# A macaron layer on one core: the opening stages of the kernel laid out anew

## Chip, cores and metric

One core of a Trainium2 chip runs the whole kernel in one launch. The metric is the device time in microseconds (us) of that core; the time of a kernel is the median of its runs. Lower is better.

## What is computed

The input x has 8 batches of 512 rows with 512 columns, all in float32. Each batch goes through three residual steps:

```
x = x + 0.5 * ffn(layernorm(x), W1, W2, W3)
x = x + attention(layernorm(x), qkv_w, proj_w, norm weights, s)
x = x + 0.5 * ffn(layernorm(x), W1, W2, W3)

ffn(x):  hidden = silu(x @ W1.T) * (x @ W3.T)      # 512 x 2048
         hidden = fwht(hidden)                     # Walsh-Hadamard transform over 2048
         return hidden @ W2.T
```

The attention is a chunked one with a decay per head (16 heads of 32, chunks of 128 rows), and its two weight matrices are rounded to -1, 0 and 1 by their mean absolute value.

## The kernel before

**Numbers.** A float32 operand is held as two float16 tiles, a high part and a low part; a product takes three matmuls (high by high, high by low, low by high), or two where the other side is exact. A group of the gate or the linear product is 12 matmuls of 128x128 by 128x512 (four tiles of the contraction by three). ScalarE makes the high part and VectorE the low part, nearly everywhere.

**The transform is moved into W2.** Since the Walsh-Hadamard transform is linear, the kernel transforms W2 once, in the opening: three butterfly stages on GpSimd (step `fly`, lines 696 to 718), then a high and a low part (`w2split`), a turn by DMA transposes into w2t, and on TensorE the last stages, as products with +1/-1 matrices over pairs of tiles (`w2pair`, lines 1342 to 1361). Pair i fills two PSUM banks with eight matmuls; ScalarE and VectorE copy them back to w2t as high and low parts (lines 791 to 795 and 1022 to 1027). Before, the pairs alternate between two bank pairs: a_bank, and g_bank with l_bank.

**One list of steps.** All engines walk the same list STEPS, written out by the Python functions first_steps and feed_forward; each engine issues its own instructions for the steps that concern it, in order, and waits on semaphores. A dictionary of slots says which steps stand at which place: slot 2j comes between gate and lin of hidden tile j, slot 2j+1 after lin j. The 16 feed-forward passes have the numbers n = 0 to 15. The opening is first_steps (lines 334 to 393):

1. W1 and W3 are loaded in 16 chunks of 128 rows (both matrices) through a stage of four. Per chunk, `wsum` takes squares on ScalarE (line 751), `wscale` makes power-of-two scales on VectorE (lines 968 to 978), `wprep` splits (lines 774 and 984), and SyncE turns the split tile by a DMA transpose (line 511) and then issues the load of the chunk that takes the free stage.
2. Layer norm of batch 0: `stat` (four bn_stats, small operations, and a power on GpSimd at line 684), `prep` (normalise one tile of 128 rows), `turn` (four float32 transposes on TensorE, line 1416, then a high part on ScalarE and a low part on VectorE).
3. Hidden stage 0 (n = 0): gate and lin groups (line 1385) for j = 0 to 15, Silu on ScalarE (line 831), the product on VectorE (`lin`, line 1102), high and low parts (lines 850 and 1109). Between them stand the preparation of later chunks, the norm of batch 1 (its rows are x_next, in the tile of mask), and, near the end, SyncE's loads of W2 (line 486), 1 MB for each of four parts.
4. Hidden stage 1 (n = 1): the same groups for batch 1, whose parts are spilled to DRAM (line 551). Between them: sums of squares of W2 (`w2sum`), the butterflies, absolute sums of the attention weights (`qsum`, line 1085, loaded in quarters at line 482), the common scales of W2 (`wtop`, `top_turn`, `top_max`, `top_spread`, `wfit`, lines 986 to 1013; f2 is scaled at line 1008), and the 16 W2 splits (lines 789 and 1019).
5. The eight W2 pairs.
6. Down projection 0 (line 1405), between whose groups stand the norm of batch 2, the decay mask, and 16 sign tiles of the attention weights (`qprep`, lines 1079 and 1080, turned at line 548), which are made in the buffer cent. Then the residual (line 1122), which frees the d_bank banks.
7. Down projection 1, with the first steps of the attention among its groups: the norm before q, k and v (it writes cent too), turned at line 642, and the first q product (line 1440).

From then on the remaining 14 passes and the attention are interleaved by feed_forward. All DMAs of these steps but two are issued by SyncE, in the order of the list.

The order of the beginning, as quoted:

```
steps = [("begin", 0), ("wsum", 0), ("wscale", 0), ("stat", key), ("wprep", 0), ("wprep", 1)]
steps += [("prep", (key, t)) for t in range(3)] + [("wsum", 1), ("turn", (key, 0)), ("prep", (key, 3))]
steps += [("turn", (key, t)) for t in range(1, TT)] + [("wscale", 1), ("wprep", 2), ("wprep", 3)]
steps += [("wsum", 2), ("wsum", 3), ("wscale", 2)]
```

## Time and profile before

| what | us |
|---|---|
| median of 3 runs | 2385.5 (2384.63 to 2386.05) |
| the profiled execution's own time | 2387.63 |
| its span, first to last instruction | 2385.9 |
| TensorE busy in the span | 2344.0 |
| VectorE busy | 1199.0 |
| ScalarE busy | 712.2 |
| GpSimd busy | 143.6 |

Times in the trace count from the span's start. PE is TensorE, PEld its weight loads, DVE is VectorE, ACT is ScalarE, POOL is GpSimd, SPq is SyncE's queue of DMA issues. A line of the timeline has the start, the time from the start of the first to the end of the last instruction of the line, engine, line of the kernel, operation, what is written and read, the count, and in brackets the idle time before it with what ended it. Ends of matmuls are modelled, so starts are compared. Tiles that share storage carry the name of the storage: the weight stage appears as w2t, x_next as mask, the split buffers as q_parts, k_parts, kT, lam_t and cent, the W2 rows as work and xt.

### The profile page before, as it was taken

To read this page: it belongs to the slowest core of one execution; us is meant where nothing else is said; L and a number is where in the kernel's file an instruction comes from. 1 tells how busy PE (TensorE), PEld (TensorE's weight loads), DVE (VectorE), ACT (ScalarE), POOL (GpSimd) and SP (SyncE) were. 2 spreads that over 40 slices of the span, in tenths; PEclk is the share of its full clock that TensorE was granted. 3 is DMA by queue.
4 is the path that set the end of the run, shared out by engine and by line. 5 is a ranking of instruction groups with operands and counts; after the bars stand their busy time and mean duration, and the time that the engine had idled before them with its cause. 6 is when DMAs were issued, how large, how long until landed. Compare 5 with 4: busy or idle time off the path is not lost.

```text
span 2385.9 us, 31855 instructions
## 1 busy us (share of the span) xinstructions
PE 2344.0 (98%) x12851; PEld 1121.7 (47%) x12851; DVE 1199.0 (50%) x2145; ACT 712.2 (30%) x1196; POOL 143.6 (6%) x102
## 2 busy tenths in 40 slices
PE   6999999999999999999999999999999999999999
PEld 3444445444444455444544454455445544544444
DVE  6576645554465445545455355534564455444312
ACT  5645333222232332223222332222233213322211
POOL 0090000000000000000000000000000000000000
PEclk9999999999999999999999999999999999999999
DMA  7947531242223322333142133411332223131210
GB/s 198 228 142 190 137 106 45 67 119 54 63 48 113 74 49 62 93 75 85 32 126 60 54 80 81 105 45 36 106 80 69 65 54 98 27 89 29 60 36 18
DMA packets 299460, 196.87 MB, mean 83 GB/s; under 512 B 231601, under 2 KB 256177, under 8 KB 295473
## 3 DMA queue, kind: packets, MB, share of 16 engines
q1 hardware_dynamic: 299024, 194.31, 31.4%
q8 instruction: 101, 1.65, 0.3%
q10 hardware_dynamic: 288, 0.52, 0.1%
q14 instruction: 47, 0.38, 0.0%
HBM read 84.68 MB, written 54.53 MB: 58 GB/s over the span
## 4 chain that ended last, share of the span: by engine, by line
PE 86%; DVE 3%; issue 3%; DMA 2%; POOL 2%; ACT 1%; SPq 1%; DVEq 0%; ACTq 0%; POOLq 0%
PE d_bank L1405 25%; PE l_bank L1385 24%; PE g_bank L1385 24%; PE a_bank L1440 5%; PE a_bank L1423 2%; PE a_bank L1499 2%; PE a_bank L1487 2%; PE a_bank L1451 1%; POOL work L714 1%; PE a_bank L1481 1%; POOL work L713 1%; DVE work L1122 1%; PE a_bank L1465 1%; DMA w1t<-kT 0%; DMA parts_dram<-q_parts 0%
## 5 line engine op out<-in xcount | busy, mean ns | idle before, releaser
L1405 PE MATMUL d_bank<-w2t,work 128*128 128x512 f16 x2940 | 673.7, 380 | 1.5 <-DVE work L1122 1.5
L1102 DVE SCALAR_TENSOR_TENSOR work<-l_bank,l_scale,work 128x512 f32<-128x512 f32 x256 | 191.7, 749 | 574.3 <-PE l_bank L1385 573.9
L1405 PEld LDWEIGHTS d_bank<-w2t,work 128*128 128x128 f16 x2940 | 285.1, 98 | 335.4 <-issue 4.3
L1385 PE MATMUL g_bank<-xt,w1t 128*128 128x512 f16 x1536 | 354.1, 380 | 4.7 <-DMA w1t<-q_parts 1.9
L1385 PE MATMUL l_bank<-xt,w3t 128*128 128x512 f16 x1536 | 352.4, 379 | 1.7 <-DVE work L1102 1.3
L831 ACT ACTIVATE work<-g_bank,g_scale 128x512 f32<-128x512 f32 x256 | 175.4, 685 | 503.5 <-PE g_bank L1385 497.1
L1385 PE MATMUL l_bank<-work,w3t 128*128 128x512 f16 x1344 | 308.4, 379 | 0.2 <-DVE work L1102 0.2
L1385 PE MATMUL g_bank<-work,w1t 128*128 128x512 f16 x1344 | 308.3, 379 | 0.0
L850 ACT CAST work<-work 128x512 f16<-128x512 f32 x232 | 143.3, 618 | 520.7 <-DVE work L1102 519.2
L1385 PEld LDWEIGHTS g_bank<-xt,w1t 128*128 128x128 f16 x1536 | 147.6, 98 | 181.0 <-issue 4.7
L1385 PEld LDWEIGHTS l_bank<-xt,w3t 128*128 128x128 f16 x1536 | 147.6, 98 | 175.7 <-issue 1.8
L1385 PEld LDWEIGHTS l_bank<-work,w3t 128*128 128x128 f16 x1344 | 129.6, 98 | 152.6 <-DVE work L1102 0.7
L1385 PEld LDWEIGHTS g_bank<-work,w1t 128*128 128x128 f16 x1344 | 129.7, 98 | 152.1
L1109 DVE TENSOR_TENSOR work<-work 128x512 f16<-128x512 f32 x232 | 160.3, 691 | 63.5 <-ACT work L850 62.9
L858 ACT CAST cent<-cent 128x512 f16<-128x512 f32 x124 | 76.6, 618 | 205.8 <-DVE cent L1219 66.2
L1288 DVE TENSOR_TENSOR work<-work 128x512 f16<-128x512 f32 x128 | 88.6, 692 | 87.5 <-ACT work L914 87.5
L1440 PE MATMUL a_bank<-zt,wqkv 128*128 128x512 f16 x512 | 120.9, 379 | 1.2 <-DMA zt<-cent 1.2
L914 ACT CAST work<-work 128x512 f16<-128x512 f32 x128 | 79.1, 618 | 116.8 <-DVE work L1283 115.2
L1239 DVE TENSOR_TENSOR cent<-cent 128x512 f16<-128x512 f32 x124 | 85.4, 689 | 42.8 <-ACT cent L858 40.8
L694 POOL TENSOR_TENSOR work<-qT,lam_t 128x512 f32<-128x512 f32 x32 | 40.7, 1272 | 1080.7 <-ACT qT L874 1080.7
L684 POOL TENSOR_TENSOR rstd<-veps,half 128x4 f32<-128x4 f32 x32 | 37.1, 1161 | 909.2 <-DVE veps L1167 544.8
L1283 DVE SCALAR_TENSOR_TENSOR work<-a_bank,mask 128x512 f32<-128x512 f32 x128 | 87.6, 684 | 4.6 <-PE a_bank L1451 4.6
(216 smaller groups left out, 1699.6 us busy)
## 6 DMA issues: line engine op xcount, KB each, us to landing
work<-parts_dram SPq DMA_DIRECT2D x192, 128.0 KB, 2.8
x_dram<-work SPq DMA_DIRECT2D x16, 1024.0 KB, 4.6
work<-x_dram SPq DMA_DIRECT2D x11, 1024.0 KB, 7.1
parts_dram<-q_parts SPq DMA_DIRECT2D x32, 256.0 KB, 2.0
parts_dram<-k_parts SPq DMA_DIRECT2D x32, 256.0 KB, 2.2
norm_dram<-cent SPq DMA_DIRECT2D x32, 256.0 KB, 2.0
w2t<-in_L_ffn_W_dram SPq DMA_DIRECT2D x30, 256.0 KB, 3.4
xin<-in_L_attn_x_dram SPq DMA_DIRECT2D x7, 1024.0 KB, 7.6
```

The costliest lines, as they stand in the source:

```text
L831: nc.scalar.activation(gate, g_bank[:], ACT.Silu, scale=g_scale[:, j:j + 1]).then_inc(gate_ready, 1)
L850: nc.scalar.copy(parts[:, 0, :], hfull).then_inc(hi_ready, 1)
L858: nc.scalar.copy(halves[:, t % 2, 0, :], centred).then_inc(ln_hi, 1)
L914: nc.scalar.copy(sc[:, c % 2, 0], flow.rearrange("p (h t) -> p h t", h=HG)).then_inc(sc_hi, 1)
L1102: nc.vector.scalar_tensor_tensor(out=hfull, in0=l_bank[:], scalar=l_scale[:, j:j + 1], in1=gate, op0=ALU.mult, op1=ALU.mult).then_inc(hful ...
L1109: nc.vector.tensor_tensor(parts[:, 1, :], hfull, parts[:, 0, :], ALU.subtract).then_inc(lo_ready, 1)
L1239: nc.vector.tensor_tensor(halves[:, t % 2, 1, :], centred, halves[:, t % 2, 0, :], ALU.subtract).then_inc(ln_lo, 1)
L1283: nc.vector.scalar_tensor_tensor(out=masked, in0=a_bank[b][:].rearrange("p (h t) -> p h t", h=HG), scalar=SCORE_SCALE, in1=mask[:, HG * g: ...
L1288: nc.vector.tensor_tensor(sc[:, c % 2, 1], masked, sc[:, c % 2, 0], ALU.subtract).then_inc(sc_lo, 1)
L1385: ins = nc.tensor.matmul(dst[:], wt[:, wp, k, P * j:P * (j + 1)], src[:, xp, k, :], start=(k == 0 and wp == xp), stop=(k == KT - 1 and wp ...
L1405: ins = nc.tensor.matmul(d_bank[t][:], parts[:, hp, P * t:P * (t + 1)], w2t[:, j, wp, :], start=(j == 0 and hp == wp), stop=(j == HT - 1 a ...
L1440: ins = nc.tensor.matmul(a_bank[b][:], wqkv[:, k, col:col + P], zt[:, part, k, :], start=(k == 0 and part == 0), stop=(k == KT - 1 and par ...
```

## The change

It touches only the opening. The two-pair rotation of banks for the W2 pairs becomes one of four (d_bank 0 and 1, d_bank 2 and 3, a_bank, g_bank with l_bank), with the waits to match. At the start, a Silu on one column is issued ahead of everything on ScalarE; a new step `rows` takes one bn_stats of the norms of batches 0 and 1, and for batch 0 it stands ahead of the weight scales, for batch 1 the four stand at slots 7, 9, 11 and 13, and the rest of that norm at slots 14 to 24 instead of 10 to 20. The load of x_next is issued after the fourth turned weight tile, and the four W2 loads after chunk 14 (first part) and chunk 15 (the other three), instead of 13, 14 and 15. In stage 1 the steps of the W2 scale stand up to one slot earlier, its f2 and unscale part becomes a step of its own (`wrest`) at slot 29, and the splits stand about one slot earlier. Four of the 16 sign tiles move from down projection 0 into the first two groups of down projection 1.

```
-        pair_bank = [a_bank, [g_bank, l_bank]]
+        pair_bank = [d_bank[0:2], d_bank[2:4], a_bank, [g_bank, l_bank]]
...
-            steps = [("begin", 0), ("wsum", 0), ("wscale", 0), ("stat", key), ("wprep", 0), ("wprep", 1)]
-            steps += [("prep", (key, t)) for t in range(3)] + [("wsum", 1), ("turn", (key, 0)), ("prep", (key, 3))]
-            steps += [("turn", (key, t)) for t in range(1, TT)] + [("wscale", 1), ("wprep", 2), ("wprep", 3)]
-            steps += [("wsum", 2), ("wsum", 3), ("wscale", 2)]
+            steps = [("begin", 0), ("wsum", 0), ("wsum", 1)] + [("rows", (key, t)) for t in range(TT)]
+            steps += [("stat", key), ("wscale", 0), ("prep", (key, 0)), ("prep", (key, 1)), ("wprep", 0), ("prep", (key, 2))]
+            steps += [("turn", (key, 0)), ("prep", (key, 3)), ("turn", (key, 1)), ("wprep", 1)]
+            steps += [("turn", (key, t)) for t in range(2, TT)] + [("wsum", 2), ("wscale", 1), ("wprep", 2), ("wprep", 3)]
+            steps += [("wsum", 3), ("wscale", 2)]
...
+            for t in range(TT):
+                add(own, 7 + 2 * t, [("rows", (("ffn1", 1), t))])
             for i, part in enumerate(norm_steps(("ffn1", 1))):
-                add(own, 10 + 2 * i, part)
+                add(own, 14 + 2 * i, part)
...
-            for at, step in ((9, "wtop"), (10, "top_turn"), (11, "top_max"), (12, "top_spread"), (13, "wfit")):
+            for at, step in ((8, "wtop"), (10, "top_turn"), (10, "top_max"), (12, "top_spread"), (12, "wfit"), (29, "wrest")):
                 add(own, at, [(step, 0)])
-            splits = (14, 16, 18, 20, 21, 22, 23, 24, 25, 25, 26, 26, 27, 27, 28, 28)
+            splits = (13, 15, 17, 19, 20, 21, 22, 23, 23, 24, 24, 25, 25, 26, 26, 27)
...
-                add(own, 7 + i, [("qprep", 2 * i), ("qprep", 2 * i + 1)])
+                if i < 6:
+                    add(own, 7 + i, [("qprep", 2 * i), ("qprep", 2 * i + 1)])
...
                 if j < 2:
-                    steps += [("reload", 7 + j)]
+                    steps += [("qprep", 12 + 2 * j), ("qprep", 13 + 2 * j), ("reload", 7 + j)]
...
-            sp.dma_start(x_next, x[1].rearrange("(t p) d -> p t d", p=P)).then_inc(x_next_loaded, 16)
...
+                    if arg == 3:
+                        sp.dma_start(x_next, x[1].rearrange("(t p) d -> p t d", p=P)).then_inc(x_next_loaded, 16)
-                    if m and c >= 13:
-                        for t in ((0,), (1,), (2, 3))[c - 13]:
+                    if m and c >= 14:
+                        for t in ((0,), (1, 2, 3))[c - 14]:
                             load_w2(t, 0)
                             load_w2(t, 1)
...
+            nc.scalar.activation(tiny[:, 15:16], ident[:, 0:1], ACT.Silu)
             act.wait_ge(dve_const, 1)
...
                 elif step == "w2pair":
+                    if arg == 0:
+                        act.wait_ge(w2_f, 2)
...
-                    nc.vector.tensor_scalar(w2_scale[:], tiny[:, 5:6], PRE_SCALE, None, ALU.mult)
+                    nc.vector.tensor_scalar(w2_scale[:], tiny[:, 5:6], PRE_SCALE, None, ALU.mult).then_inc(w2_f, 1)
+                elif step == "wrest":
+
                     link(power(tiny[:, 4:5], top_all[:, 0:1], True))
...
+                elif step == "rows":
+
+                    (kind, batch), t = arg
+                    if batch:
+                        dve.wait_ge(x_next_loaded, 16 * batch)
+                    else:
+                        dve.wait_ge(x_first[t], 16)
+                    nc.vector.bn_stats(stat[:, t, :], norm_source(arg[0])[:, t, :]).then_inc(ln_stats, 1)
...
-                    elif i == 1:
+                    elif i == 3:
 
                         pe.wait_ge(gate_ready, 2 * HT)
                         pe.wait_ge(hfull_ready, 2 * HT)
-                    else:
-
-                        pe.wait_ge(w2_final_lo, 2 * (i - 1))
+                    elif i >= 4:
+
+                        pe.wait_ge(w2_final_lo, 2 * (i - 3))
...
                     if n == 0:
 
-                        pe.wait_ge(w2_final_lo, 2 * j + 1 if j < HT // 2 else HT)
+                        pe.wait_ge(w2_final_lo, max(2 * j + 1, 12) if j < HT // 2 else HT)
```

## Rows read from the trace of the kernel before

**Rows 1.** The page, busy time by engine: busy us (share of the span) xinstructions.
```profile
PE 2344.0 (98%) x12851; PEld 1121.7 (47%) x12851; DVE 1199.0 (50%) x2145; ACT 712.2 (30%) x1196; POOL 143.6 (6%) x102
```

**Rows 2.** TensorE's waits, 0 to 330 us: us in total, times, longest us.
```profile
PE l_bank L1385 <- DVE work L1102: 3.9, 4, 2.4
```

**Rows 3.** The start: x's tile with its landing, then the timeline to 27 us.
```profile
L489 SPq DMA_DIRECT2D xin<-in_L_attn_x_dram x4: 395/426/432, 0.8 to 2.2; - x4
...
DMA to landing us min/median/max: 4.0/5.0/5.3
...
6.39 1.28 ACT L751 ACT_TABLE_LOAD   x1 [6.39 <-DMA w2t<-in_L_ffn_W_dram]
...
10.00 2.46 DVE L1147 BATCH_NORM_STATS2 stat<-xin 128x6 f32<-128x512 f32 x4
...
14.91 1.46 DVE L1224 TENSOR_SCALAR cent<-xin,mean,rstd 128x512 f32<-128x512 f32 x3 [0.26 <-POOL rstd L684]
...
21.85 4.44 PE L1385 MATMUL g_bank<-xt,w1t 128*128 128x512 f16 x12 [1.52 <-issue]
...
26.87 1.28 ACT L831 ACT_TABLE_LOAD   x1
```

**Rows 4.** TensorE's timeline at the end of hidden stage 0.
```profile
102.21 2.76 PE L1385 MATMUL g_bank<-xt,w1t 128*128 128x512 f16 x12 [1.49 <-DMA w1t<-q_parts]
...
108.00 2.76 PE L1385 MATMUL g_bank<-xt,w1t 128*128 128x512 f16 x12 [0.44 <-DMA w1t<-kT]
...
113.19 2.75 PE L1385 MATMUL g_bank<-zt,w1t 128*128 128x512 f16 x12
```

**Rows 5.** The 32 turned weight tiles of line 511: time from issue to landing.
```profile
DMA to landing us min/median/max: 3.0/3.7/6.6
```

**Rows 6.** Hidden stage 1 from 152 us: timeline; the fifth line is of the windows view.
```profile
152.31 2.15 DVE L1008 TENSOR_SCALAR f<-f,tiny 128x16 f32<-128x16 f32 x1
...
156.82 2.67 POOL L713 TENSOR_TENSOR work<-work 128x1024 f32<-128x1024 f32 x1
157.21 2.83 DVE L1019 SCALAR_TENSOR_TENSOR kT<-xt,w_scale,kT 128x512 f16<-128x512 f32 x1
...
160.75 4.28 PE L1385 MATMUL l_bank<-zt,w3t 128*128 128x512 f16 x12 [2.42 <-DVE work L1102]
...
162.00:163.00 1.00, 1.00 (x4) 0.30 (x2) 1.00 (x2) 0.55 (x1) 0.86 (x2) 0.50 0.74 135
...
176.01 2.82 POOL L714 TENSOR_TENSOR work<-work 128x1024 f32<-128x1024 f32 x1
176.52 0.74 DVE L1102 SCALAR_TENSOR_TENSOR work<-l_bank,l_scale,work 128x512 f32<-128x512 f32 x1
...
177.99 2.75 PE L1385 MATMUL l_bank<-zt,w3t 128*128 128x512 f16 x12
...
178.57 0.80 DVE L1019 SCALAR_TENSOR_TENSOR kT<-work,w_scale,kT 128x512 f16<-128x512 f32 x1 [1.31 <-ACT kT L789]
```

In the windows line the column after the five engines is the granted TensorE clock, then the share of the DMA engines and GB/s.

**Rows 7.** Timeline of the W2 pairs and the two down projections.
```profile
202.94 1.89 PE L1359 MATMUL a_bank<-w2t,hadamard 128*128 128x512 f16 x8 [1.07 <-DMA w2t<-cent]
...
205.59 1.41 DVE L1026 SCALAR_TENSOR_TENSOR w2t<-a_bank,f,w2t 128x512 f16<-128x512 f32 x2 [1.56 <-ACT w2t L794]
...
218.77 15.70 PE L1405 MATMUL d_bank<-w2t,wqkv 128*128 128x512 f16 x72
...
258.84 0.42 DVE L1079 TENSOR_SCALAR cent<-work 128x512 f16<-128x512 f32 x1
...
260.35 0.69 DVE L1080 SCALAR_TENSOR_TENSOR cent<-work,cent 128x512 f16<-128x512 f32 x1
...
261.85 3.40 PE L1405 MATMUL d_bank<-w2t,work 128*128 128x512 f16 x15 [1.48 <-DVE work L1122]
...
281.75 1.25 SPq L642 DMA_TRANSPOSE zt<-cent  x1
...
292.93 1.89 PE L1440 MATMUL a_bank<-zt,wqkv 128*128 128x512 f16 x8
```

More of the change, by code:

```diff
@@ L1025, in _ @@
                         dve.wait_ge(w2_final_hi, 2 * arg + half + 1)
-                        nc.vector.scalar_tensor_tensor(out=w2t[:, j, 1, :], in0=pair_bank[arg % 2][half][:], scalar=f2[:, j:j + 1],
+                        nc.vector.scalar_tensor_tensor(out=w2t[:, j, 1, :], in0=pair_bank[arg % 4][half][:], scalar=f2[:, j:j + 1],
                                                        in1=w2t[:, j, 0, :], op0=ALU.mult, op1=ALU.subtract).then_inc(w2_final_lo, 1)
@@ L1143, in _ @@
                             dve.wait_ge(a_free[b], copied("proj", (batch, t), b) + 1)
-                    for t in range(TT):
-                        if m == 0:
-                            dve.wait_ge(x_first[t], 16)
-                        nc.vector.bn_stats(stat[:, t, :], src[:, t, :]).then_inc(ln_stats, 1)
+                    if kind != "ffn1" or batch > 1:
+                        for t in range(TT):
+                            nc.vector.bn_stats(stat[:, t, :], src[:, t, :]).then_inc(ln_stats, 1)
                     dve.wait_ge(ln_stats, TT * (m_ln + 1))
```

4 lines of the change are left out of this document (2 added, 2 removed).

## The prediction

> **What bounds the kernel now.** I read the page first: TensorE is busy for 98% of the span [rows 1], so the kernel is bound by TensorE, and only what shortens its idle or slow stretches can count. The list of TensorE's waits over the first 330 us shows, after the start, four waits of 3.9 us in sum for VectorE to free l_bank as the largest [rows 2]. I then followed TensorE in the timeline and compared starts. A group of 12 matmuls takes 2.6 us at full pace (108.00 to 113.19 are two groups) [rows 4], one matmul 0.216 us. The stages lose this: the first group starts at 21.85 [rows 3]; hidden stage 0 runs from there to 113.19, 91.3 us for 32 groups of 2.6 us, 8.3 lost; hidden stage 1 runs to the first W2 pair at 202.94, 89.75 us, 6.7 lost; the pairs run to 218.77 [rows 7], 15.8 us for 64 matmuls worth 13.8, 2.0 lost; down projection 0 runs to 261.85, 43.1 us for 192 matmuls worth 41.5, 1.6 lost. After that nothing of the change runs. So 21.85 + 18.6 us are all that it can work on.
>
> **Opening.** The statistics of x start at 10.00 although the last tile of x was issued at 2.2 us and a tile took 4.0 to 5.3 us to land, so it was there at 7.5 at the latest [rows 3]. Ahead of them on VectorE stood the scale of W1's first chunk, which needs two squares on ScalarE, and these began only after a table load of 1.28 us at 6.39. With the statistics first, they start at about 6 and, with the last tile at 7.5, end at 8.2. Before, 14.91 minus 12.46 = 2.45 us went by from their end to the first normalised tile, so that tile comes at 10.7, now with the first scale computed under GpSimd's power: 4.2 us earlier than 14.91. From there to the first group it was 6.94 us, with three tiles prepared ahead of the first turn. Now only two stand there, but the two weight splits of VectorE (0.74 each, as the like instruction at 176.52 [rows 6]) come between the turns; the one more or less cancels the other and I take 6.7, so the first group starts at 17.4. **Gain 4.4**, bounds 3.0 (the splits cost 1.5 in full) and 4.8. The table load at 6.39 moves to a time when ScalarE waits for data, and the second one at 26.87 goes altogether, since the squares after 26.87 brought no further load, so the Silu set serves them too [rows 3]; that one made the first Silu late and is in the sum of stage 0.
> The Trainium skill (ScalarE: Activation LUTs, What ACT_TABLE_LOAD costs) puts a switch at 2.66 us with its drain; the trace has 1.28 for the load and no further gap, and by the page's figure each of the two would give back 1.4 us more.
>
> **Stage 0 (8.3 lost).** The first group is slow (4.44 against 2.75 [rows 3, 4]): 1.7, which stays. The groups at 102.21 and 108.00 wait for turned weights, 2.25 by their starts. They do so because turned tiles, which take 3.0 us to land at best, take up to 6.6 behind 1 MB of W2 [rows 5]: the one for 108.00 was issued at 101.4. The first of the two W2 loads moves one chunk later, so the wait at 102.21 goes; but the second chunk's turned tile then has 1 MB ahead of it as before, is issued at about the same 101.4 to 101.7, since it follows the Silu of group 13, and is needed 1.6 us earlier, at 105.8. The wait moves: 2.5 in place of 2.25. The other 4.35 are small waits. The late Silu after 26.87 makes about 1.0, the four statistics in one block (2.46 us of VectorE) 1.2; of the waits on VectorE in [rows 2] 1.5 belong here. One statistic at a time (0.6) fits into a step of 5.2, so these 2.2 go. The norm's other steps move two steps later, where SyncE has fewer chunk loads to issue; I leave 1.2 of the 2.15 that remain. The new place of x's load costs: 1 MB and a chunk's 0.5 MB now stand ahead of the turned tile for gate 2, issued at about 24. With 6.6 to 8 us to land that is 30.6 to 32, needed at 29.5: 1.5 lost, bounds 0 and 3. Sum 1.7 + 2.5 + 1.2 + 1.5 = 6.9: **gain 1.4**.
>
> **Stage 1 (6.7 lost).** Here VectorE and GpSimd alternate. GpSimd runs butterflies of 2.35 to 2.82 us back to back until 178.83. A VectorE instruction with two SBUF inputs, 0.7 alone, ends 0.55 us after GpSimd's current one: the first split of W2 runs 157.21 to 160.04, while GpSimd ended at 159.49 [rows 6]. So each such instruction costs a GpSimd turn of some 2.75 us (the row at 176.01 has 2.82), and one j of stage 1 with a low half and a split costs 5.5, more than TensorE's 5.2. The scale of f2 (2.15 at 152.31) cost a turn too. That made l_bank free only at 160.7, a wait of 2.42, and the group after it ran with the granted clock at 0.50, 4.28 instead of 2.75 [rows 6]. Together that is 4.0 us.
> The change takes the f2 work out, and the splits start one slot earlier. What stands ahead of f2 today ends at 152.3, and the same stands ahead of the first split then; after lin a split waits 1.31 for ScalarE's copies (178.57 [rows 6]), so it asks at 153.6. GpSimd's turns end at 154.4, where f2 ends now, 157.2, 159.9 and so on; with split and low half done at 157.7, lin 7 is done at 158.4 instead of 160.7, and the wait of 2.42 shrinks to 0.3. But count the instructions that need a turn between lin 6 and lin 10: before, f2, four low halves and four splits, nine; after, four low halves and five splits, nine. So lin 10 comes at 176.9 against 176.52, and TensorE, earlier now (six groups after 158.5, with 0.7 of small waits, is 174.8), waits about 3.0 before group lin 11, which starts at 177.8 against 177.99 [rows 6]. The wait is moved, not removed, and 3.0 is more than the 2.42 that brought the clock down, so I add 1.6 for a slow group. After GpSimd's end all is as before, less 0.4 of small waits, since the splits are over sooner. 177.8 less 177.99, and 1.6 less 0.4: **loss 1.0**; bounds: gain 4.4 (no wait at either place), loss 4 (missed turns, below). Quarter 0 of the qkv weights is loaded behind 1 MB more and may be 3.6 us late; the wait at lin 11 hides what it costs.
> The last W2 split moves from slot 28 to 27, 2.6 us, and the wait of 1.07 for its landing [rows 7] is gone: **gain 1.25** with the gap around it, bounds 0 and 1.25.
>
> **Pairs.** With four bank pairs pair i waits for pair i-4's copies instead of i-2's. VectorE, the last to empty a pair, needs 1.41 us for its two copies and is done 2.3 after TensorE (202.94 + 1.73 to 207.00) [rows 7]; TensorE needs 1.73 for a pair, so no wait is left: **gain 2.0**. The new wait of down 0 for 12 copies is for pair 5, which ends 3.5 us ahead of pair 7, and its copies are done in 2.3: no cost; bounds gain 1.0 (half of the waits return, as one wait ahead of down 0) and 2.0.
>
> **Sign tiles.** In down 0 VectorE works through tiles (two instructions each, 0.42 and 0.69; the last two tiles from 258.84 to 261.04), and only then, at 261.04, adds the residual that frees d_bank; so TensorE waits 1.48 [rows 7]. Bank 0 was complete nine matmuls ahead of the end, at 258.3. Four tiles fewer are 4.3 us, VectorE is free at 256.8, and the residual starts on time: **gain 1.6**. The tiles now stand behind the residual, ahead of the qkv norm, and behind 2 MB of stores and loads in the queue. By 3.6 us for each MB (6.6 less 3.0 [rows 5]) they land at about 272.5, the norm follows, its last turned tile goes out at 283.5 to 286 (before 281.75) and lands by 287 to 292.6; the q product needs it at 291.3 (292.93 less 1.6) [rows 7]. No cost in the likely case, 1.3 at the bad end.
>
> **Sum.** 4.4 + 1.4 - 1.0 + 1.25 + 2.0 + 1.6 = 9.65 us. The profiled execution took 2387.63 (span 2385.9), 2.1 above the median of 2385.5; from its own time the change leads to 2378.0, from the median to **2375.9**. What follows 292 is bound by TensorE and shifts as a whole.
>
> **Rivals.**
> (a) The stall of stage 1 really goes. For it: lin 7 comes 2.3 us earlier. Against: nine turns before and nine after. It would give 1.0 + 4.4 more, 2370.5. Chance 0.14.
> (b) Missed turns. In the new order the split waits for two ScalarE copies and asks 0.5 + 0.74 + 1.31 = 2.55 us after the last turn ended, where turns are 2.6 to 2.9 apart. Each miss costs 2.75 until GpSimd ends at 178.83, and what is left then takes 0.75 each, so at most some 3 us: 2378.5. Chance 0.23.
> The Trainium skill (SBUF — State Buffer, SBUF: two separate sides) has the shared port pair as an exclusive lock, kept for the whole instruction, the loser blocking fully. By that rule VectorE loses whole turns as in (b); the trace agrees for VectorE (ends 0.55 after GpSimd's end) but not for GpSimd, whose next instruction starts at once.
> (c) Most of it is given back: the x load costs 1.5 more, the last split is late (1.25), the opening wins only 3.0, and one turn is missed (2.75). Then 2.75 us are left, 2382.7, no change that can be told. Chance 0.10.
> (d) Slower: the sign tiles. They hold the buffer that the qkv norm writes, and stand behind 2 MB. If they land after 276.8 (272.5 and the 4.3 that the norm has to spare), each us later holds TensorE one us at the first q product. At 286.4 the gain is used up, at 291.3 the kernel is slower by 4.9: 2390.4. Landing then would be 29 us after the issue, where no turned tile of W1 took over 6.6 [rows 5]. Chance 0.03.
> My forecast has 0.50.
>
> **Chances and range.** 0.2% are 4.8 us, about what a measurement of this kernel tells from no change. Forecast, (a) and (b) are faster by more: 0.87. (c): 0.10 within. (d): 0.03. The range from 2370 to 2381 takes in (a), (b) and the bounds of single terms; outside are (c) and (d), and the outer ends of (a) and (b).
>
> **What would show it.** Right: the first gate group at 17.4; one table load before 6 us and none at the first Silu; a wait before gate 2 or 3 for turned weights; no wait at gate 14 and about 2 us at gate 15; the longest wait for VectorE at lin 11 in place of lin 8, with GpSimd's end as far from the start of stage 1 as now (65.6 us); the eight pairs in 13.9 us; no wait of TensorE for the residual. Wrong: stage 1 shorter than 86 us (then turns are not what paces it), or TensorE waiting at the first q product.

## The result, and the profile after it

The changed kernel takes **2391.79 us** (median of 19 runs, 2388.42 to 2395.56). The kernel before, run in turn with it, takes 2387.44 (19 runs, 2384.39 to 2388.48). The ratio of the two is 1.0019 (95% interval 1.0012 to 1.0025): the change makes the kernel slower by 4.4 us. The prediction was 2375.9, faster. It was wrong in sign and by 15.9 us.

The page after the change, busy time by engine, answers to [rows 1]:

```profile
PE 2345.6 (98%) x12851; PEld 1123.4 (47%) x12851; DVE 1199.4 (50%) x2145; ACT 710.3 (30%) x1196; POOL 142.7 (6%) x102
```

The counts are those of before: the one Silu that the change adds on ScalarE stands against one table load fewer. So every difference is one of order and waiting. TensorE's waits from 0 to 330 us (us in total, times, longest us), against [rows 2]:

```profile
PE l_bank L1401 <- DVE work L1111: 7.9, 8, 2.5
PE d_bank L1375 <- DVE w2t L1035: 5.9, 1, 5.9
PE g_bank L1401 <- DMA w1t<-q_parts: 2.1, 1, 2.1
```

The wait for VectorE to free l_bank was to shrink or move; it has doubled, from 3.9 to 7.9. And there are two new ones, which the prediction had as no wait at all (5.9) and as 1.5 (2.1). As before the change, I cut TensorE's timeline into stages by the starts of its groups. The last column but one is the start of the first q product, behind which nothing of the change runs:

| us | first group at | stage 0 | stage 1 | W2 pairs | down 0 to first q product | first q product at | span |
|---|---|---|---|---|---|---|---|
| before | 21.85 | 91.34 | 89.75 | 15.83 | 74.16 | 292.93 | 2385.9 |
| after | 17.52 | 93.54 | 93.60 | 21.42 | 72.52 | 298.60 | 2390.5 |
| gain | 4.33 | -2.20 | -3.85 | -5.59 | 1.64 | -5.67 | -4.6 |
| predicted gain | 4.4 | 1.4 | 0.25 | 2.0 | 1.6 | 9.65 | 9.65 |

(The prediction's stage 1 is its loss of 1.0 and its gain of 1.25 for the last split together, since both lie ahead of the first pair.) Both ends of the change, the opening and the sign tiles, do what was forecast. The middle loses 11.6 us in place of gaining 3.65. The profiled execution took 2392.25, 1.75 above its span. After the first q product 1.1 us come back (5.67 against 4.6).

**The pairs.** The timeline of TensorE from the first pair to the fifth answers to the first half of [rows 7]. Columns: start, length, engine, line, what it writes and reads, count, and in brackets the wait before it and what ended it.

```profile
204.66 3.62 PE L1375 MATMUL d_bank<-w2t,hadamard 128*128 128x512 f16 x16
208.12 1.89 PE L1375 MATMUL a_bank<-w2t,hadamard 128*128 128x512 f16 x8
209.84 1.03 PE L1375 MATMUL g_bank<-w2t,hadamard 128*128 128x512 f16 x4
210.71 1.03 PE L1375 MATMUL l_bank<-w2t,hadamard 128*128 128x512 f16 x4
217.63 5.16 PE L1375 MATMUL d_bank<-w2t,hadamard 128*128 128x512 f16 x16 [5.90 <-DVE w2t L1035]
```

Pairs 0 to 3 run without a gap, over all eight banks. Then pair 4 waits 5.90 for pair 0's copies, and the 16 matmuls behind the wait take 5.16 in place of 3.62 (the granted clock is 0.50 from 217.6 to 220.0, the 1.2 GHz level). 5.90 and 1.54 are 7.44 of the 7.6 by which this stage misses 13.8. What VectorE and ScalarE were doing, by their timelines:

```profile
214.91 0.62 ACT L857 CAST k_parts<-work 128x512 f16<-128x512 f32 x1 [11.95 <-DMA hid_dram<-k_parts]
215.44 2.42 ACT L801 ACTIVATE w2t<-d_bank,f 128x512 f16<-128x512 f32 x4
...
215.56 0.69 DVE L1118 TENSOR_TENSOR k_parts<-work,k_parts 128x512 f16<-128x512 f32 x1 [9.95 <-ACT k_parts L857]
216.17 2.72 DVE L1035 SCALAR_TENSOR_TENSOR w2t<-d_bank,f,w2t 128x512 f16<-128x512 f32 x4
```

Neither had been busy before these lines. ScalarE stood for 11.95 us before the high part of hidden tile 15, because the buffer k_parts still had to be stored: that is tile 13's spill store. The pair copies stand behind that cast in ScalarE's program, and VectorE's low part, which waits for the cast, stands ahead of its own copies. SyncE's timeline shows why a store that lands in 2 to 3 us took so long (length is time on the queue):

```profile
197.29 2.86 SPq L540 DMA_TRANSPOSE w2t<-cent  x2
200.19 1.71 SPq L544 DMA_DIRECT2D work<-in_L_attn_qkv_w_dram  x3
201.94 0.65 SPq L544 DMA_DIRECT2D work<-in_L_attn_proj_w_dram  x1
202.63 3.03 SPq L555 DMA_DIRECT2D hid_dram<-k_parts  x1
```

The last W2 split ends with SyncE issuing the four weight tiles of the attention layer, 1 MB each. With the split one slot earlier they are issued ahead of tile 13's store. Before the change the same view has that store ahead of them, and the one behind them is that of tile 14, whose buffer no later tile needs:

```profile
197.56 0.58 SPq L551 DMA_DIRECT2D hid_dram<-k_parts  x1
198.18 2.67 SPq L536 DMA_TRANSPOSE w2t<-cent  x2
200.90 1.70 SPq L540 DMA_DIRECT2D work<-in_L_attn_qkv_w_dram  x3
202.64 0.65 SPq L540 DMA_DIRECT2D work<-in_L_attn_proj_w_dram  x1
203.34 3.03 SPq L551 DMA_DIRECT2D hid_dram<-q_parts  x1
```

The store that stands behind the loads takes 12.2 us from issue to landing in both kernels; only in one does anybody wait for it. For the kernel after, the view of the spill tensor says so:

```profile
who waited for it (us, times):
  ACT k_parts L857: 11.9, 1
...
DMA to landing us min/median/max: 2.0/3.0/12.2
```

The Trainium skill (DMA: Bandwidth & Descriptors, Two DMAs through the same engine are not ordered) says that in one queue of one DMA engine the transfers start in the order of issue. The trace agrees: a store that lands in 2.0 us at best landed after 12.2 with 4 MB ahead of it in the queue.

**Stage 1.** All its waits of over 0.4 us on TensorE, from its timeline:

```profile
141.77 2.76 PE L1401 MATMUL l_bank<-zt,w3t 128*128 128x512 f16 x12 [1.52 <-DVE work L1111]
...
148.77 2.76 PE L1401 MATMUL l_bank<-zt,w3t 128*128 128x512 f16 x12 [1.34 <-DVE work L1111]
...
154.67 2.76 PE L1401 MATMUL l_bank<-zt,w3t 128*128 128x512 f16 x12 [0.55 <-DVE work L1111]
...
161.07 2.76 PE L1401 MATMUL l_bank<-zt,w3t 128*128 128x512 f16 x12 [1.05 <-DVE work L1111]
...
168.88 4.45 PE L1401 MATMUL l_bank<-zt,w3t 128*128 128x512 f16 x12 [2.45 <-DVE work L1111]
```

Five waits, from lin 5 to lin 9, 6.9 us in sum, with 1.7 for the slow group behind the last. The prediction had only one of 0.3 before lin 11. VectorE's timeline shows where they come from. (A GpSimd turn is one instruction of GpSimd, at whose end VectorE gets on.)

```profile
137.14 2.31 DVE L996 TENSOR_TENSOR f<-k_turned_parts 128x16 f32<-128x16 f32 x1
...
145.07 1.87 DVE L1005 TENSOR_SCALAR cent<-ident,tops 2x2 f32<-2x2 f32 x1
...
155.92 1.46 DVE L1028 SCALAR_TENSOR_TENSOR kT<-xt,w_scale,kT 128x512 f16<-128x512 f32 x1 [1.31 <-ACT kT L794]
157.30 2.83 DVE L1118 TENSOR_TENSOR q_parts<-work,q_parts 128x512 f16<-128x512 f32 x1
160.26 0.75 DVE L1111 SCALAR_TENSOR_TENSOR work<-l_bank,l_scale,work 128x512 f32<-128x512 f32 x1
162.32 2.87 DVE L1028 SCALAR_TENSOR_TENSOR lam_t<-xt,w_scale,lam_t 128x512 f16<-128x512 f32 x1 [1.31 <-ACT lam_t L794]
165.11 2.82 DVE L1118 TENSOR_TENSOR k_parts<-work,k_parts 128x512 f16<-128x512 f32 x1
```

The first two are steps of the W2 scale that moved from slots 9 and 11 to 8 and 10. An instruction on 128x16 elements takes 2.31 us and one on 2x2 elements 1.87; before they took 0.54 and 0.09. They sit under GpSimd's instructions 136.63 to 139.42 and 144.29 to 146.91, and end with them. So did the one of 0.54 in the kernel before; only, GpSimd's instruction had 0.51 us left when it started:

```profile
138.73 2.82 POOL L714 TENSOR_TENSOR work<-work 128x1024 f32<-128x1024 f32 x1
...
141.04 0.54 DVE L989 TENSOR_TENSOR f<-k_turned_parts 128x16 f32<-128x16 f32 x1
```

The one of 0.09 started 0.06 us before GpSimd's instruction ended. Each of these costs what is left of GpSimd's turn, however small it is itself. In the kernel after they are ahead of the instruction that frees l_bank (L1111), so lin 5 and 6 wait. Further on the split of lam_t asks at 162.32, GpSimd's instruction having started at 162.30, and waits out a whole turn; the low part behind it takes the next one, and lin 9 waits 2.45. GpSimd's last instruction ends at 175.84, 64.8 us after the start of stage 1 (65.6 before).

**Stage 0.** The start on TensorE, against [rows 3]:

```profile
17.52 5.28 PE L1401 MATMUL g_bank<-xt,w1t 128*128 128x512 f16 x12 [1.52 <-issue]
...
32.72 4.45 PE L1401 MATMUL g_bank<-xt,w1t 128*128 128x512 f16 x12 [2.09 <-DMA w1t<-q_parts]
```

and its end, against [rows 4]:

```profile
98.09 2.75 PE L1401 MATMUL g_bank<-xt,w1t 128*128 128x512 f16 x12
101.89 2.76 PE L1401 MATMUL l_bank<-xt,w3t 128*128 128x512 f16 x12 [1.05 <-DMA w3t<-k_parts]
105.87 2.76 PE L1401 MATMUL g_bank<-xt,w1t 128*128 128x512 f16 x12 [1.22 <-DMA w1t<-kT]
```

### The profile page after: what moved, and what is told of

Its sections match the earlier page's. It is cut to its first block, busy times and chain, and to the rows that moved or that the text cites. A ratio compares the mean times of both kernels' runs of the same rounds, so it can differ in the third digit from the quotient of the medians.

```text
span 2390.5 us, 31856 instructions
## 1 busy us (share of the span) xinstructions
PE 2345.6 (98%) x12851; PEld 1123.4 (47%) x12851; DVE 1199.4 (50%) x2145; ACT 710.3 (30%) x1196; POOL 142.7 (6%) x102
## 3 DMA queue, kind: packets, MB, share of 16 engines
q8 instruction: 101, 1.65, 0.3%
## 4 chain that ended last, share of the span: by engine, by line
PE 90%; DVE 5%; DMA 3%; ACT 1%; SPq 1%; issue 1%; POOL 0%; DVEq 0%; ACTq 0%; POOLq 0%
PE d_bank L1421 26%; PE l_bank L1401 25%; PE g_bank L1401 25%; PE a_bank L1456 5%; PE a_bank L1439 2%; PE a_bank L1515 2%; PE a_bank L1503 2%; PE a_bank L1467 1%; PE a_bank L1497 1%; DVE work L1131 1%; DVE work L1111 1%; PE a_bank L1481 1%; DMA hid_dram<-k_parts 1%; DMA w1t<-kT 0%; DMA parts_dram<-q_parts 0%
## 5 line engine op out<-in xcount | busy, mean ns | idle before, releaser
L1111 DVE SCALAR_TENSOR_TENSOR work<-l_bank,l_scale,work 128x512 f32<-128x512 f32 x256 | 191.8, 749 | 574.9 <-PE l_bank L1401 574.4
```

Of the source, the lines that this page charges most:

```text
L1111: nc.vector.scalar_tensor_tensor(out=hfull, in0=l_bank[:], scalar=l_scale[:, j:j + 1], in1=gate, op0=ALU.mult, op1=ALU.mult).then_inc(hful ...
```

## The experiments

Unless it says otherwise, an edit is against the kernel after, and the stages are read from one profiled execution each. All of them:

| us | first group at | stage 0 | stage 1 | pairs | first q product at | span |
|---|---|---|---|---|---|---|
| last split back in slot 28 (a1) | 17.40 | 91.43 | 93.52 | 13.81 | 288.68 | 2382.3 |
| attention weights from the first pair (a2) | 17.62 | 90.49 | 92.63 | 13.81 | 287.07 | 2378.6 |
| a2, with scale and splits in their old slots (a3) | 17.40 | 93.32 | 88.03 | 13.81 | 285.08 | 2376.4 |
| a2, next x loaded early (a4) | 17.40 | 88.83 | 93.55 | 13.82 | 286.12 | 2380.1 |
| a3 and a4 together (a5) | 17.45 | 89.02 | 88.04 | 13.81 | 280.84 | 2373.1 |
| before, with four bank pairs (b1) | 21.12 | 92.91 | 89.01 | 13.81 | 290.76 | 2383.8 |
| before, with sign tiles later (b2) | 21.07 | 91.53 | 89.04 | 15.83 | 289.99 | 2385.0 |
| before, last two splits in slot 27 (d1) | 21.65 | 93.40 | 89.65 | 27.74 | 306.53 | 2399.6 |
| a2, scale in its old slots (c1) | 17.40 | 93.29 | 92.43 | 13.81 | 289.45 | 2383.0 |
| a2, splits in their old slots (c2) | 17.55 | 91.00 | 91.23 | 13.81 | 286.11 | 2379.9 |
| a5, W2 loads in their old places (e1) | 17.41 | 90.33 | 88.04 | 13.81 | 282.11 | 2373.8 |
| a5, all W2 loads behind chunk 15 (e2) | 17.40 | 88.35 | 88.67 | 13.81 | 280.75 | 2372.8 |

### The last split alone

```
-            splits = (13, 15, ..., 25, 25, 26, 26, 27)
+            splits = (13, 15, ..., 25, 25, 26, 26, 28)
```

> The changed kernel with one number changed: the last of the 16 W2 splits stands at slot 28 again, instead of 27. Theory Q (queue): with the last split at slot 27, SyncE issues the 4 MB of attention weights that follow it ahead of the spill store of hidden tile 13; ScalarE's last high part, which overwrites that store's source, waits 11.95 us, the copies of the W2 pairs queue behind it, and TensorE waits 5.90 us before pair 4 and then runs a slow stretch. Q expects: no wait of ScalarE over 1 us there, the eight pairs in 13.9 to 14.5 us instead of 21.4, up to 1.3 us of wait for the last turned W2 tile ahead of pair 0, 6.3 us less than the changed kernel, about 2 us less than the kernel before (ratio 0.999). Rival R (banks): the rotation through four bank pairs itself makes the wait, since d_bank is freed late; then the wait of 5.9 stays and the time is that of the changed kernel, 4.4 over before.

Measured: 2382.54 us (2379.96 to 2386.3, 11 runs), ratio to before 0.998 (0.9971 to 0.9988). One number in a list turns 4.4 us slower into 4.5 faster (its kernel before took 2387.07). The pairs on TensorE:

```profile
202.35 3.62 PE L1375 MATMUL d_bank<-w2t,hadamard 128*128 128x512 f16 x16
205.80 1.89 PE L1375 MATMUL a_bank<-w2t,hadamard 128*128 128x512 f16 x8
207.53 1.03 PE L1375 MATMUL g_bank<-w2t,hadamard 128*128 128x512 f16 x4
208.39 1.03 PE L1375 MATMUL l_bank<-w2t,hadamard 128*128 128x512 f16 x4
209.25 3.62 PE L1375 MATMUL d_bank<-w2t,hadamard 128*128 128x512 f16 x16
```

Pair 4 follows pair 3 at once, and the whole stage takes 13.81, its matmul time. Pair 0 does not wait for the landing of the last split either, though that split is in slot 28 again: with stage 1 as long as here, the tile has landed by then.

The reverse, in the kernel before, where pairs go through two bank pairs:

```
-            splits = (..., 25, 25, 26, 26, 27, 27, 28, 28)
+            splits = (..., 25, 25, 26, 26, 27, 27, 27, 27)
```

> The kernel before with its last two W2 splits at slot 27 instead of 28, nothing else. Theory Q: this alone makes the attention weight loads go out ahead of the spill store of hidden tile 13, so ScalarE waits about 10 to 12 us for it and TensorE 7 or more in the pairs, of which only two fit into the banks: pairs 23 to 27 us instead of 15.8, kernel 7 to 11 us slower than before (ratio 1.003 to 1.0045). Rival R: the place of the split is harmless, the time is that of before.

Measured: 2399.89 us (2399.28 to 2401.32, 4 runs), ratio 1.0048 (1.0033 to 1.0063), 12.5 over its kernel before (2387.39) and somewhat more than the 7 to 11 expected.

```profile
218.70 3.60 PE L1359 MATMUL a_bank<-w2t,hadamard 128*128 128x512 f16 x8 [10.38 <-DVE w2t L1026]
```

The wait moves to pair 2, the first that needs copies there, and is 10.38 long, and ScalarE waits 13.0 for the store of k_parts. So the queue stall needs nothing else of the change, and the four bank pairs hide part of it (5.90 in place of 10.38): here the pairs take 27.74, 11.9 more than before, where in the changed kernel they take 7.6 more than without the stall. The wait for the landing at pair 0 is gone here, but gate 15 waits 2.04 for ScalarE, so the earlier splits did not make stage 1 shorter (89.65).

### The four bank pairs alone, in the kernel before

```
-        pair_bank = [a_bank, [g_bank, l_bank]]
+        pair_bank = [d_bank[0:2], d_bank[2:4], a_bank, [g_bank, l_bank]]
...
-                        pe.wait_ge(w2_final_lo, 2 * (i - 1))
+                        pe.wait_ge(w2_final_lo, 2 * (i - 3))
```

> The kernel before with the four bank pairs alone (the rotation and its waits, nothing else). Theory Q: without the reordered queue the rotation does what it should: pairs in 13.8 us instead of 15.8, all else equal, 2.0 us less than before (ratio 0.9992). Theory R (the banks make the wait): pairs as long as before or longer, time not lower.

Measured: 2385.21 us (2384.37 to 2388.4, 11 runs), ratio 0.9992 (0.9983 to 1.0001), which by itself is not told from no change. The stage tells it: 13.81 in place of 15.83, with the pairs in an unbroken row as in a1. That refutes the rival that the long wait of pair 4 came with the new banks or with their new wait counts, and confirms the 2.0 of the prediction.

### The sign tiles alone, in the kernel before

```
-                add(own, 7 + i, [("qprep", 2 * i), ("qprep", 2 * i + 1)])
+                if i < 6:
+                    add(own, 7 + i, [("qprep", 2 * i), ("qprep", 2 * i + 1)])
...
-                    steps += [("reload", 7 + j)]
+                    steps += [("qprep", 12 + 2 * j), ("qprep", 13 + 2 * j), ("reload", 7 + j)]
```

> The kernel before with the four sign tiles moved alone. Expected by the prediction's step: no wait of TensorE for the residual (1.48 now), no new wait at the first q product, 1.6 us less from the start of down projection 0 to the first q product (72.5 instead of 74.2), ratio 0.9993. Rival: the norm of the attention is late and TensorE waits at the first q product; then 74 or more stay.

Measured: 2386.32 us (2383.7 to 2388.58, 11 runs), ratio 0.9995 (0.9986 to 1.0003), again not told from no change by the time. In the trace the wait of 1.48 at 261.85 [rows 7] is gone, and the first q product waits for nothing:

```profile
271.86 18.29 PE L1406 MATMUL d_bank<-w2t,work 128*128 128x512 f16 x84
289.99 1.89 PE L1441 MATMUL a_bank<-zt,wqkv 128*128 128x512 f16 x8
```

The stretch from down 0 to the first q product takes 72.52 in place of 74.16. In it 1.64 are gained, and rival (d) is refuted.

### The loads out of the split

The four loads of the attention weights are issued with the first pair instead of behind the last split:

```
                 elif step == "w2split":
...
-                    if arg == KT * CHUNKS - 1:
-                        for w in range(FOURTHS):
-                            sp.dma_start(wst[:, 4 * w:4 * w + 4, :], quarter(w)).then_inc(wst_loaded[w], 16)
+                elif step == "w2pair":
+                    if arg == 0:
+                        for w in range(FOURTHS):
+                            sp.dma_start(wst[:, 4 * w:4 * w + 4, :], quarter(w)).then_inc(wst_loaded[w], 16)
```

> The changed kernel, with the last split left at slot 27, but the four attention weight loads (4 MB) issued after the last spill store, at the step of the first W2 pair. Q expects: every spill store ahead of the loads, pairs in 13.9 us, no wait ahead of pair 0, 7.5 us less than the changed kernel, about 3 us less than before (ratio 0.9987). R expects the wait of 5.9 to stay. Either: if the loads now come too late for the scaling of the attention weights in down projection 0, a new wait of ScalarE appears there, hidden from TensorE.

Measured: 2383.42 us (2380.3 to 2387.24, 11 runs), ratio 0.9985 (0.9976 to 0.9994). The pairs take 13.81 with the last split still in slot 27: what hurts is not the split but the 4 MB that hang on it. No new wait of ScalarE for these weights appears in down projection 0. The time is within the scatter of a1's.

### Scale and splits in their old slots

On a2:

```
-            ((8, "wtop"), (10, "top_turn"), (10, "top_max"), (12, "top_spread"), (12, "wfit"), (29, "wrest"))
+            ((9, "wtop"), (10, "top_turn"), (11, "top_max"), (12, "top_spread"), (13, "wfit"), (29, "wrest"))
...
-            splits = (13, 15, 17, 19, 20, 21, 22, 23, 23, 24, 24, 25, 25, 26, 26, 27)
+            splits = (14, 16, 18, 20, 21, 22, 23, 24, 25, 25, 26, 26, 27, 27, 28, 28)
```

> As the run with the late weight loads, and in hidden stage 1 the steps of the W2 scale at slots 9, 10, 11, 12, 13 and the 16 splits at slots 14 to 28 as before (the f2 part stays at slot 29). Theory T (turns): in hidden stage 1 every VectorE instruction with two SBUF inputs, or of the kind that the small W2 scale steps have, costs a GpSimd turn; moved one slot earlier, two small ones (the product for f2 at 2.31 us, the scalar product for the top pair at 1.87 us) fell ahead of a lin and held l_bank, which made stage 1 93.6 us against 89.75 to the first pair. T expects 88 to 89.5 us from the first gate group of stage 1 to the first pair, 4 to 5 us less than the run with the late loads, ratio to before about 0.9967. Rival N: stage 1 is longer because the attention weights of the first quarter come later or because of where stage 1 starts; then the old slots leave it at 92 to 94 us.

Measured: 2377.6 us (2373.95 to 2379.46, 5 runs), ratio 0.9955 (0.9942 to 0.9967). Stage 1 takes 88.03: 4.60 less than in a2, and 1.72 less than before the change. Of the 1.72 only 1.0 can be told from chance: b1 and b2, alike with the kernel before in this stage, took 89.01 and 89.04 in it, with its wait at lin 8 (2.43 and 2.42) but without the slow group behind it. The f2 work is still out of the way (wrest stays in slot 29), and that is a gain once nothing else is moved. (The last split is in slot 28 again, too, but with the attention loads hanging on the first pair that slot matters only for its landing: pair 0 waits 0.93.) To see which of the two lists costs, each alone. First a2 with only the scale in its old slots:

> As the run with the late weight loads, with the steps of the W2 scale back at slots 9, 10, 11, 12, 13 and the splits left where the change put them (13 to 27). It parts theory T: if the small scale steps ahead of a lin make stage 1 long, it falls here from 92.6 to 93.5 us to 88 to 89.5. If the split between lin and its low half does (it asks for GpSimd's turn after two ScalarE copies), stage 1 stays at 91 or more.

Measured, one run: 2384.77 us (before on the same chip 2385.76), stage 1 92.43. TensorE's waits there:

```profile
163.98 2.76 PE L1402 MATMUL l_bank<-zt,w3t 128*128 128x512 f16 x12 [2.47 <-DVE work L1112]
...
177.91 4.27 PE L1402 MATMUL l_bank<-zt,w3t 128*128 128x512 f16 x12 [2.87 <-DVE work L1112]
```

The early waits are gone, and so are the long small instructions behind them. VectorE:

```profile
138.54 0.54 DVE L997 TENSOR_TENSOR f<-k_turned_parts 128x16 f32<-128x16 f32 x1
...
144.17 0.09 DVE L1006 TENSOR_SCALAR cent<-ident,tops 2x2 f32<-2x2 f32 x1
```

What is left, 2.47 at lin 9 and 2.87 at lin 11, is of the splits. The second, with its slow group, is what the prediction had at lin 11 (a wait of 3.0 and 1.6 for a slow group); the first it did not have. Then a2 with only the splits in their old slots:

> As the run with the late weight loads, with the splits back at slots 14 to 28 and the scale steps left where the change put them (8, 10, 10, 12, 12). The mirror of the run before: small scale steps to blame, stage 1 stays at 91 or more; the split's place to blame, it falls to 88 to 89.5. Both in part: each of the two runs lies between.

Measured, one run: 2381.61 us, stage 1 91.23:

```profile
139.33 2.76 PE L1402 MATMUL l_bank<-zt,w3t 128*128 128x512 f16 x12 [1.52 <-DVE work L1112]
...
146.34 2.76 PE L1402 MATMUL l_bank<-zt,w3t 128*128 128x512 f16 x12 [1.34 <-DVE work L1112]
```

The two waits of the small instructions stand exactly as in the kernel after, and no wait for l_bank after 160 is over 0.2. So the slots of the scale make the early waits, those of the splits the late ones; neither list put back alone brought the stage to the 88 to 89.5 expected of the one to blame. With the other list old, the new scale slots cost 3.20 (91.23 less 88.03) and the new split slots 4.40 (92.43 less 88.03); together they cost 4.60, not 7.6. These are single profiles, and 1.5 of the 4.40 is c1's slow group, which neither a2 nor c2 has. For the rest my reading is that it is one sequence of turns, and that a turn lost early shifts the phase of all that follow; no run of its own tests that.

### The load of the next x

On a2, the load goes back behind the first chunk loads:

```
             for j in range(1, STAGES):
                 load_chunk(j)
+            sp.dma_start(x_next, ...).then_inc(x_next_loaded, 16)
...
-                    if arg == 3:
-                        sp.dma_start(x_next, ...).then_inc(x_next_loaded, 16)
```

> As the run with the late weight loads, and the load of the next x (1 MB) issued behind the first weight chunks as before, instead of behind the fourth turned tile. Theory X: the wait of 2.09 us at gate 2 and the slow group after it (4.28 against 2.59) come from this 1 MB standing ahead of the turned tile. X expects both gone, hidden stage 0 in 89.5 to 90 us instead of 93.5, the first gate group at 17.5 to 18, 3.9 us less than the run with the late loads. Rival: the tile is late because its own split is late (ScalarE and VectorE in the opening); then the wait stays at 1 to 2 us.

Measured: 2381.84 us (2378.72 to 2385.14, 11 runs), ratio 0.9976 (0.9967 to 0.9985); a2 has 0.9985 (0.9976 to 0.9994). It is 1.6 less than a2, where 3.9 was expected. Gate 2 no longer waits and runs at full pace; in the kernel after it started at 32.72:

```profile
29.49 2.75 PE L1401 MATMUL g_bank<-xt,w1t 128*128 128x512 f16 x12
```

In the kernel after, the turned tile for gate 2 was issued at 25.00, behind the 1 MB of x at 23.55, and took 7.7 us to land. How much that costs differs between executions. The six profiles with x late (after, a1, a2, a3, c1, c2) all wait at gate 2, for 1.79 to 2.58. In three of them the group behind the wait is slow, and the first group of the stage was long:

| us | after | a3 | c1 | a1 | a2 | c2 |
|---|---|---|---|---|---|---|
| first group | 5.28 | 5.28 | 5.00 | 4.17 | 4.49 | 4.78 |
| wait before gate 2 | 2.09 | 2.23 | 2.40 | 2.58 | 1.79 | 2.16 |
| group of gate 2 | 4.45 | 4.45 | 4.26 | 2.76 | 2.76 | 2.76 |
| stage 0 | 93.54 | 93.32 | 93.29 | 91.43 | 90.49 | 91.00 |

So the same wait costs about 2 or about 4. In these six the slow group goes with a first group of 5.00 or more, but the granted clock is 1.00 from 22 to 32 us in all of them, so no row ahead of the wait says why. The mean of stage 0 is 92.18 with x late; with x early and nothing else different in the stage it took 88.83 here and 89.02 in a5 below, some 3 us less. The medians of the timed runs show less: 1.6 from a2 to a4 and 1.25 from a3 to a5, with intervals that overlap.

### Both repairs together

a3 and a4 in one kernel: the attention weights from the first pair, the old slots, x early; kept of the change are the opening, the later W2 loads, f2 in slot 29, the four bank pairs and the later sign tiles.

> The changed kernel with three things set right at once: attention weight loads after the last spill store, W2 scale and split slots as before, next x loaded at the start. If the three causes are apart and add: first gate group at 17.4, stage 0 88.8 us, stage 1 88.0 us, pairs 13.8, 72.5 to the first q product, together 280.6 against 292.9 before: 12.3 us less, near 2375, ratio 0.9948. Rival (they share one cause, the start of stage 1 against GpSimd or the DMA queue): stage 1 is 90 us or more again with the shorter stage 0.

Measured: **2376.35 us** (2374.88 to 2377.84, 5 runs), ratio 0.995 (0.9938 to 0.9963), 11.0 under its kernel before (2387.39) and 15.4 under the change as it came. It beats both. Its first q product starts at 280.84, 12.1 earlier than before the change.

### The places of the W2 loads

On a5, the loads of W2 behind chunks 13, 14 and 15, as before the change:

```
-                    if m and c >= 14:
-                        for t in ((0,), (1, 2, 3))[c - 14]:
+                    if m and c >= 13:
+                        for t in ((0,), (1,), (2, 3))[c - 13]:
```

> The best version so far (late attention weight loads, old slots of stage 1, next x at the start) with the W2 loads where they were before the change (after chunks 13, 14 and 15). The prediction had the wait at gate 14 only moved to gate 15 by the change, so hidden stage 0 should be equal within 0.3 us: 88.5 to 89.1. If the change's later W2 loads do win, it is 1 to 2 us longer here.

Measured, one run: 2375.52 us (before on the same chip 2385.76), stage 0 90.33 against a5's 89.02. TensorE waits 2.90 at gate 14 for a turned tile behind the W2 loads; a5 waits 0.67 there, and 1.15 at gate 15, where this kernel does not wait:

```profile
95.73 4.41 PE L1401 MATMUL g_bank<-xt,w1t 128*128 128x512 f16 x12 [2.90 <-DMA w1t<-q_parts]
```

2.90 and 1.65 for the slow group, 4.55, against 1.82, is 2.7 more; some of it is made up elsewhere in the stage, and 1.3 is left. Four kernels with the stage 0 of before (before, b1, b2, d1) took 91.34, 92.91, 91.53 and 93.40 in it, so one run is a hint and no more. All four loads behind chunk 15:

```
-                    if m and c >= 14:
-                        for t in ((0,), (1, 2, 3))[c - 14]:
+                    if m and c == 15:
+                        for t in range(4):
```

> The best version so far with all four W2 loads after chunk 15. No turned weight tile has a W2 load ahead of it any more: the waits at the last gate and lin groups of stage 0 (2.6 us in sum) should go, stage 0 86.2 to 86.8 us. But W2's first part lands only at the start of stage 1, so GpSimd's first butterfly starts up to 5 us late and the W2 splits with it: stage 1 88 to 92. A gain in sum only if the second stays under 2.3.

Measured, one run: 2374.51 us, stage 0 88.35, stage 1 88.67, sum 177.02 against 177.06 in a5. The waits at gate 14, lin 14 and gate 15 are gone, but lin 13 waits 0.88 and the first group is slow (5.06), so stage 0 stays above the 86.2 to 86.8 expected. GpSimd's first butterfly does not come late (0.3 us after the start of stage 1, as in a5). What makes stage 1 longer is VectorE's first sum of the attention weights, which waits 5.20 for its load in place of 1.94; it stands ahead of the instruction that frees l_bank, and TensorE waits 1.53 at lin 2, and then 0.96 in place of 0.26 at the small matmul of the W2 scale. No gain.

## Why the prediction was wrong

**The step that failed** is "The last W2 split moves from slot 28 to 27 ... gain 1.25, bounds 0 and 1.25". The wait for the landing did go, as it said, though it is gone in a1 too, with the split back in slot 28. But what the step issues was not followed through: behind the split SyncE issues 4 MB, and the spill store of tile 13 is behind it in the same queue, with ScalarE's cast for tile 15, VectorE's low part and the copies of all pairs behind that store. a1 and d1 price it: 9.25 us between the medians of the kernel after and a1, of which 7.6 are in the pairs and the rest is not traced; in d1, 12.5, of which 11.9 are in the pairs. The trace of before has what was needed, though the prediction read no row of it: a store at 203.34, 3.03 long on the queue, right behind the 4 MB, and a longest landing of 12.2. With these 12.2 the wait comes out, if the times at which the loads end and pair 4 is due are taken from the kernel after: put behind the loads (202.6), the store of k_parts lands at 214.8; 0.6 for ScalarE's cast, 0.7 for the low part and 1.4 for a pair's copies are 217.5, and pair 4 is due at 211.6: a wait of 5.9, and 5.90 was measured. The lower bound of 0 was the error: no row stood behind it.

**Stage 1** was forecast at a loss of 1.0, with bounds of a gain of 4.4 and a loss of 4.0. Up to the first pair a2 loses 2.88 (92.63 against 89.75), although the 1.07 of the landing wait is gone; so the turns cost 3.9 to 4.0 there and 4.9 in the kernel after (3.85 and 1.07), past the bound, and 0.7 more against b1 and b2. The mechanism was half right. VectorE does lose whole turns to GpSimd, and c1 shows the wait at lin 11; but the step "nine turns before, nine after" left out the 128x16 and the 2x2 instruction of the scale, which happened to be cheap before, and it put all that is lost at one place, lin 11. The waits fall where the phase is missed, at lin 5 to 9. So rival (b), missed turns, came true, at more than its 3 us. Rival (a), the stall going altogether, was put at 4.4 better than before; with f2 moved and nothing else, it goes (no wait for l_bank over 0.82 in a3), but the stage gains only 1.72, or 1.0 against b1 and b2.

**Stage 0** was forecast at a gain of 1.4: 2.9 from the waits that go, less 1.5 for x's load. One profile against one shows a loss of 2.2, but kernels alike in this stage differ by 3.05 (x late) and by 2.06 (before), in part by whether the group behind a wait runs slow. The means are 92.18 over six and 92.30 over four: no gain that can be told. With x early it is 88.93 (a4, a5), 3.4 under before, so the 2.9 was about right, and the term that was too small is x's load: 1.5 forecast, some 3 in the profiles, 1.3 to 1.6 in the timed medians. The waits at gate 2 are 1.8 to 2.6, and the price left out is the slow group behind them, 1.5 to 1.7 in three of six. At the stage's end the waits moved as it said: in the kernel after gate 14 waits no more, lin 14 and gate 15 wait 1.05 and 1.22, 2.27 in sum against 2.5 forecast.

**Right**: the opening, 4.33 against 4.4, with the table load at 1.71 and none at the first Silu. How near it came is in part luck: the four kernels with the old opening start at 21.07 to 21.85, the ten with the new one at 17.40 to 17.62, 4.0 between the means. The four bank pairs, 2.0 (b1, and 13.81 or 13.82 in all kernels that have them but the one stalled). The sign tiles, 1.64 against 1.6 (b2), with no wait at the first q product.

**Of the rivals**, (c) had the x load and one missed turn in it, but took the split only as a gain forgone; (d) looked for the slow end at the sign tiles, 60 us behind where it was. The chance of 0.03 for slower rested on that single place. No rival asked of each moved step what stands behind it in each queue, although the term of x's load was worked out that way.

**A row misread**, without a part in the sum: beside rival (b) the prediction says that GpSimd is not held up, since its next instruction starts at once. It does start at once, but it takes longer. In the kernel before, between 100 and 185 us, the 9 butterflies at whose start no VectorE instruction with two SBUF inputs was running took 2.34 to 2.36 us, and the 14 into which one ran on for 0.4 us or more took 2.60 to 2.82. So each of the two holds the other up.

**Accounted for**: from 2391.79, the queue gives 9.25 (a1), the old slots 5.8 (a2 to a3), x early 1.3 to 1.6, less 0.9 between a1 and a2 that is within scatter: 2376.35. The opening, the later norm of batch 1 and the later W2 loads were not run apart in the kernel before. **Open**: what puts the clock in the state in which a wait of 2 us costs a slow group as well, and what the later W2 loads give (1.3 in one run). The 1.1 us that come back after the first q product were not followed.

## What to carry to other kernels

When a step is moved by one slot, list all that it issues, on every queue, and for each queue name the first thing that is passed; if a small store passes behind megabytes of loads, ask whose buffer it frees and who waits for that buffer. A prefetch that nobody needs soon should not hang on a step that is placed for other reasons. Where VectorE and GpSimd take turns, the price of a VectorE instruction is its phase, not its size: judge a new order of small steps by a run, not by a count of turns.

## What the runs showed that was not expected

- A VectorE instruction on 2x2 elements takes 0.09 us or 1.87, one on 128x16 takes 0.54 or 2.31, by how much of a GpSimd instruction of 2.35 to 2.8 us is left when it starts; in all four cases it ends within 0.03 us of that instruction. The Trainium skill (SBUF — State Buffer, SBUF: two separate sides) tells of the port pair that the two engines share as a lock held for a whole instruction, whichever comes first. The traces agree with it, down to 2x2 elements, and for GpSimd too, whose butterflies take 0.25 to 0.5 us more when a VectorE instruction runs into them.
- A store of a tile that takes 2.0 us at best took 12.2 behind 4 MB in the same queue, and a turned tile 7.7 behind 1 MB and a chunk, where 3.0 is the least.
- A wait of TensorE can cost more than its length. In the kernel after, the groups behind its waits of 2.09, 2.45 and 5.90 us took 4.45, 4.45 and 5.16, for what takes 2.76, 2.76 and 3.62, with the granted clock between 0.50 and 0.67 in the 2 us from their start; behind 1.52 and 1.34 they did not. Around 2 us it is not the wait's length that decides: at gate 2 a wait of 2.09 was followed by a slow group and one of 2.58 by none, and in stage 1 a wait of 2.47 by a slow one in a4 (4.45) and by none in a2 and c1 (2.76).
